# A transformer block with eight experts on one core: the experts' second product as three fp32r products in place of one fp32 product

## The chip, the cores and the metric

The kernel runs on one core of a Trainium2 chip. The time is that of one execution on the device, in microseconds (us). All times of instructions below come from one profiled execution.

## What is computed

The input is x, 4 batches of 1,024 rows of 128 numbers (4,096 tokens). After a layer norm with scale and shift, attention with 16 heads, a second layer norm and a router, every token goes to two of eight experts; each expert takes at most 1,280 rows. An expert is

```python
pre = jnp.einsum('ech,edh->ecd', expert_inputs, ff_pre_act_weight)
gate = jnp.einsum('ech,edh->ecd', expert_inputs, gate_weight)
expert_out = jnp.einsum('ecd,ehd->ech', pre * jax.nn.silu(gate), ff_post_act_weight)
```

with c = 1,280 rows, h = 128 and d = 512. The outputs are weighted, added up per token, multiplied by a gate and added to x. All of it is float32. The change concerns the last einsum alone, called the second product below; the first two are the gate product and the up product.

## The kernel before, in words

The program is written out by hand for each engine, and the engines meet at semaphores. Until 740 us it does the norms, the attention and the router; then come the eight experts, and after them a last stage that gathers the sums and writes the output. Only the expert stage is touched.

An expert e works on its rows in three parts n = 0, 1, 2 of 512, 512 and 256 rows (`CH`, line 36), and on its 512 hidden numbers in four pieces f of 128 (`FC`, line 35). Buffers alternate: q = e % 2 for weights and rows, f % 2 for the silu's result, and the two PSUM banks of the up and gate products.

TensorE (`expert`, line 1075) does, for each expert: `up(e, q, 0)`, `up(e, q, 1)`, `down` of part 0, `up(e, q, 2)`, the transposes of the next expert's rows for its parts 0 and 1 (`turn_rows`, line 1041), `down` of part 1, the transposes for part 2, `down` of part 2. It does not stop between two experts: `up(e + 1)` stands right behind.

- `up` (line 1050) makes, for each f, the gate product and then the up product. So an f is six fp32r matmuls (line 1047) with the weights as the stationary operand, 128 columns wide, and 512 or 256 rows moving. The gate product of f waits for the silu of f - 2, the up product of f for the hidden product of f - 2, since two PSUM banks of each are there.
- `down` (line 1064) is the second product: for each tile of 128 rows, four fp32 matmuls (line 1071) over f add up in PSUM. The hidden numbers of the tile are the stationary operand (128 columns), the 128 columns of w2 move. It waits for `hid_ready`, the hidden product of the part's last f, and for `y_ready`, that the PSUM bank was read. The trace shows each of these fp32 matmuls as two instructions, each with a weight load of its own (320 in the program, 640 in the trace).

ScalarE (`expert`, line 1255): for each f a silu of the gate product (line 1244, PSUM to `sg`, called hT in the trace); after a second product `results_out` (line 1251) weights its tiles into `yo`; it makes the high parts of the next expert's rows (line 1234) and, at the very end of expert e, of the first weights of expert e + 2 (`high_weights`, line 1223, 1,024 columns).

VectorE (`expert`, line 1749): for each f the hidden product hid = up x silu (line 1747, one operand in PSUM, one in SBUF), then the low parts of the next expert's rows (line 1729).

GpSimd (line 730): per expert ten indirect DMAs (line 725) that add a tile of 128 result rows each into the sums in DRAM, then `low_weights` (line 688), the low part of the first weights of expert e + 2, an SBUF subtraction of 1,024 columns. Ahead of the last stage it waits for nothing else; the last stage starts when the last of these DMAs has landed (line 451).

SyncE (line 438) loads the weights and rows of expert e + 2. The second weights w2 go to columns 1,024 to 1,535 of `w_raw` (called early in the trace), once the last second product of expert e has read them (line 448).

## Time and profile before

| | |
|---|---|
| median of three runs | 979.72 us |
| the three runs | 968.63, 979.72, 982.14 us |
| profiled execution | 973.02 us |
| its span, first to last instruction | 971.3 us |
| TensorE busy | 729.5 us (75%) |
| VectorE busy | 567.2 us (58%) |
| ScalarE busy | 460.5 us (47%) |
| GpSimd busy | 394.0 us (41%) |
| mean granted TensorE clock | 0.84 of full speed |
| first gate product of expert 0 | starts at 740.3 us |
| last second product of expert 7 | ends at about 937.5 us |

The span is read from the first instruction's start to the last one's end. PE is TensorE's matmuls and PEld its weight loads, DVE is VectorE, ACT ScalarE, POOL GpSimd, SP and SPq SyncE and its DMA queue. The duration of a matmul runs from its issue to the end of its results, so the durations of neighbours overlap; what one costs in a stream is the distance from its start to the start of the next.

### The profile page before, as it was taken

What the parts mean: (1) busy time and instruction counts of PE and PEld (TensorE: products, weight loads), DVE (VectorE), ACT (ScalarE), POOL (GpSimd) and SP (SyncE); (2) the same over time, 40 slices, a digit from 0 to 9 for tenths busy, and PEclk for the clock granted to TensorE, in tenths of its full rate; (3) what the DMA queues carried; (4) which work ended last, traced back from release to release, by engine and by line L of the source; (5) the groups of instructions that cost most, each with busy time, mean ns of one, the idle gap of its engine ahead of it and who ended that gap; (6) DMA issues with size and microseconds to landing.
All of it is one profiled execution on the core that took longest, in us unless ns stands there. A gap on an engine that the chain in (4) does not pass through costs nothing.

```text
span 971.3 us, 17136 instructions
## 1 busy us (share of the span) xinstructions
PE 729.5 (75%) x5876; PEld 395.5 (41%) x5876; DVE 567.2 (58%) x1066; ACT 460.5 (47%) x903; POOL 394.0 (41%) x432
## 2 busy tenths in 40 slices
PE   4654888888978747879876897975306999999960
PEld 2331233333423212334321342321304889889850
DVE  6859578888878925787763787720512333333314
ACT  2440467767756515756533765563103444444420
POOL 5550121113432341253151343255460677777762
PEclk9875599999979757998865998795656999999985
DMA  4255633451100111001010100000014454443326
GB/s 119 78 170 166 120 72 70 89 104 35 35 16 21 46 33 37 19 17 35 28 38 15 33 3 2 1 21 26 0 39 110 85 89 87 86 86 38 28 28 178
DMA packets 68177, 55.97 MB, mean 58 GB/s; under 512 B 7040, under 2 KB 58752, under 8 KB 68096
## 3 DMA queue, kind: packets, MB, share of 16 engines
q1 hardware_dynamic: 54528, 45.40, 17.9%
q0 software_dynamic: 13568, 9.51, 7.0%
q8 instruction: 48, 0.79, 0.3%
q14 instruction: 33, 0.27, 0.1%
HBM read 29.19 MB, written 25.31 MB: 56 GB/s over the span
## 4 chain that ended last, share of the span: by engine, by line
PE 58%; DVE 12%; ACT 9%; issue 7%; DMA 5%; another core or an unknown queue 4%; POOL 3%; SPq 2%; DVEq 0%; ACTq 0%; POOLq 0%
PE psum L847 15%; PE psum L832 13%; PE psum L1047 11%; PE psum L1071 7%; ACT prob_all L1189 7%; PE psum L807 5%; DVE mx L1381 2%; DMA k_parts<-prob_all 2%; PE psum L856 2%; DVE xn L1322 1%; PE psum L815 1%; SPq L365 1%; POOL slot_rows L622 1%; PE psum L885 1%
## 5 line engine op out<-in xcount | busy, mean ns | idle before, releaser
L1189 ACT ACTIVATE prob_all<-psum 128x512 f32<-128x512 f32 x576 | 318.0, 598 | 247.0 <-PE psum L832 205.7
L1381 DVE TENSOR_REDUCE mx<-psum 128x2 f32<-128x1024 f32 (+3 forms) x384 | 347.3, 953 | 141.4 <-PE psum L815 58.4
L832 PE MATMUL psum<-stack 51*128 51x512 bf16 (+3 forms) x768 | 199.9, 362 | 83.9 <-ACT prob_all L1189 64.0
L637 POOL TENSOR_SCALAR_AFFINE_SELECT prob_all<-prob_all 128x512 f32<-128x512 f32 x128 | 79.0, 635 | 395.5 <-ACT prob_all L1189 395.5
L807 PE MATMUL psum<-stack 48*128 48x512 bf16 (+3 forms) x768 | 165.6, 370 | 20.5 <-DVE mx L1381 11.7
L847 PE MATMUL psum<-prob_all,vst 128*32 128x512 f32 (+3 forms) x1536 | 180.2, 570 | 0.3 <-POOL prob_all L637 0.2
L725 POOL DMA_INDIRECT sums<-ys,dest_of x80 | 124.0, 1550 | 80.9 <-ACT ys L1251 53.0
L832 PEld LDWEIGHTS psum<-stack 51*128 51x128 bf16 x768 | 49.3, 96 | 256.2 <-ACT prob_all L1189 189.6
L1747 DVE TENSOR_TENSOR hid<-psum,hT 128x512 f32<-128x512 f32 (+1 forms) x96 | 57.1, 602 | 93.5 <-ACT hT L1244 66.4
L815 PE MATMUL psum<-mask_k,mask_q 64*128 64x64 bf16 x1024 | 78.0, 202 | 7.2 <-issue 7.2
L1071 PE MATMUL psum<-early,hid 128*128 128x128 f32 x640 | 75.2, 275 | 0.0
L622 POOL DMA_INDIRECT slot_rows<-early,idxb x64 | 62.8, 981 | 29.4 <-issue 19.0
L1071 PEld LDWEIGHTS psum<-early,hid 128*128 128x128 f32 x640 | 73.9, 192 | 0.6
L1047 PE MATMUL psum<-x_h,w_h 128*128 128x512 f32 (+1 forms) x192 | 71.6, 373 | 2.3 <-DVE x_l L1729 1.0
L1244 ACT ACTIVATE hT<-psum 128x512 f32<-128x512 f32 (+1 forms) x96 | 49.8, 530 | 49.6 <-PE psum L1047 45.7
L815 PEld LDWEIGHTS psum<-mask_k,mask_q 64*128 64x128 bf16 x1024 | 59.1, 104 | 29.8 <-issue 15.8
L1047 PE MATMUL psum<-x_h,w_l 128*128 128x512 f32 (+1 forms) x192 | 68.4, 356 | 0.0
L1047 PE MATMUL psum<-x_l,w_h 128*128 128x512 f32 (+1 forms) x192 | 68.4, 356 | 0.0
L807 PEld LDWEIGHTS psum<-stack 48*128 48x128 bf16 x768 | 49.4, 98 | 42.1 <-DVE mx L1381 28.6
L847 PEld LDWEIGHTS psum<-prob_all,vst 128*32 128x32 f32 x1536 | 37.9, 117 | 56.9 <-issue 50.3
L1251 ACT ACTIVATE ys<-psum,weight_of 128x128 f32<-128x128 f32 x80 | 23.2, 367 | 58.3 <-PE psum L1071 58.3
L1729 DVE TENSOR_TENSOR x_l<-psum,x_h 128x512 fp32r<-128x512 f32 (+1 forms) x24 | 13.8, 599 | 58.1 <-ACT x_h L1234 58.1
(178 smaller groups left out, 684.9 us busy)
## 6 DMA issues: line engine op xcount, KB each, us to landing
slot_rows<-fill SPq DMA_DIRECT2D x4, 1300.0 KB, 11.2
vals<-slot_rows SPq DMA_DIRECT2D x8, 650.0 KB
stack<-q_parts SPq DMA_DIRECT2D x32, 96.0 KB
stack<-k_parts SPq DMA_DIRECT2D x32, 96.0 KB
xs<-x SPq DMA_DIRECT2D x4, 512.0 KB, 6.3
stack<-q_parts SPq DMA_DIRECT2D x32, 64.0 KB
stack<-k_parts SPq DMA_DIRECT2D x32, 64.0 KB
early<-w1T SPq DMA_DIRECT2D x8, 256.0 KB
```

Of the source, the lines that this page charges most:

```text
L622: nc.gpsimd.indirect_dma_start(slot_rows, bass.IndirectOffsetOnAxis(ap=idxb[:, k, t:t + 1], axis=0), rows[:, k, t, :], None, bounds_check= ...
L637: ins = nc.gpsimd.affine_select(out=v, in_=v, compare_op=ALU.is_ge, fill=0.0, base=0, pattern=[[0, GH], [1, P]], channel_multiplier=-1)
L725: nc.gpsimd.indirect_dma_start(sums, bass.IndirectOffsetOnAxis(ap=dest_of[q][:, st:st + 1], axis=0), yo[q][:, st, :], None, bounds_check=T ...
L807: mm = nc.tensor.matmul(o, qst[buf][r, hp, i * P:i * P + P], kst[buf][r, hp, k0:k0 + w], start=True, stop=not diag, skip_group_check=True)
L815: mm = nc.tensor.matmul(o, mask_q[r, e, j, :], mask_k[r, e, j, :], start=False, stop=j == 1, skip_group_check=True)
L832: mm = nc.tensor.matmul(psum[:, KB[s % 2], col:col + w], kst[buf][r, hp, kb * P:kb * P + P], qst[buf][r, hp, qc * 512 + q0:qc * 512 + q0 + ...
L847: mm = nc.tensor.matmul(psum[32 * h:32 * h + 32, PV, q0:q0 + w], vst[buf][:, kb, h, :], probs[k % NP][:, h, col:col + w], start=kind in (0 ...
L1047: mm = nc.tensor.matmul(out_ap, left[a], right[b], start=i == 0, stop=i == 2)
L1071: mm = nc.tensor.matmul(psum[:, 6 + par, i * P:i * P + P], hid[par][:, f, i * P:i * P + P], w_raw[q][:, c:c + D], start=f == 0, stop=f == ...
L1189: nc.scalar.activation(probs[kind % NP][:, h, :], psum[:, KB[s % 2], :], ACT.Exp, scale=SCALE).then_inc(exped, 1)
L1381: ins = nc.vector.tensor_reduce(mx[:, part, :, hp, i], psum[:, QB[u % 2]:QB[u % 2] + 2, col:col + w], AX.X, ALU.max)
L1747: nc.vector.tensor_tensor(hid[par][:, f, 0:ns * P], psum[:, 2 + 2 * (f % 2), 0:ns * P], sg[f % 2][:, 0:ns * P], ALU.mult).then_inc(hid_rea ...
```

## The change

The hidden numbers and w2 are split into high and low parts as the rows and the first weights are, and `down` makes three fp32r matmuls of 128 moving columns for each fp32 matmul, with the tiles, the order over f and the PSUM bank as they were:

```diff
-        hid = [sb(f"hid{i}", [P, FC, 512]) for i in range(2)]
+        hid = [sb(f"hid{i}", [P, 512]) for i in range(2)]
+        hid_h, hid_l = ([sb(f"hid_{n}{i}", [P, FC, 512], F32R) for i in range(2)] for n in "hl")
+        w2_h, w2_l = ([sb(f"w2_{n}{i}", [P, FC * D], F32R) for i in range(2)] for n in "hl")
...
-                    sp.wait_ge(down_mm, e * 3 + 3)
+                    sp.wait_ge(w2_low, e + 1)
                     load_second_weights(e + 2, q)
...
             def down(e, q, n, par):
                 s0, ns = CH[n]
-                pe.wait_ge(hid_ready, (e * 3 + n) * FC + FC)
+                pe.wait_ge(hid_low, (e * 3 + n) * FC + FC)
                 after(pe, y_ready, e * 3 + n - 1)
+                hids, w2s = (hid_h[par], hid_l[par]), (w2_h[q], w2_l[q])
                 for i in range(ns):
                     for f in range(FC):
-                        c = 2 * F + f * D
-                        mm = nc.tensor.matmul(psum[:, 6 + par, i * P:i * P + P], hid[par][:, f, i * P:i * P + P],
-                                              w_raw[q][:, c:c + D], start=f == 0, stop=f == FC - 1)
+                        for k, (a, c) in enumerate(((0, 0), (0, 1), (1, 0))):
+                            mm = nc.tensor.matmul(psum[:, 6 + par, i * P:i * P + P],
+                                                  hids[a][:, f, i * P:i * P + P], w2s[c][:, f * D:f * D + D],
+                                                  start=f == 0 and k == 0, stop=f == FC - 1 and k == 2)
                 mm.then_inc(down_mm, 1)
...
-                pe.wait_ge(w2_in[q], j * 16 + 16)
+                pe.wait_ge(w2_low, e + 1)
                 down(e, q, 0, q)
...
+            def high_second(e, q, k):
+                act.wait_ge(w2_in[q], k * 16 + 16)
+                act.sem_inc(act_waited, 1)
+                nc.scalar.activation(w2_h[q][:], w_raw[q][:, 2 * F:3 * F], ACT.Copy).then_inc(w2_high, 1)
...
+            def high_hidden(e, n, f, par):
+                ns = CH[n][1]
+                act.wait_ge(hid_ready, (e * 3 + n) * FC + f + 1)
+                if f == 0:
+                    after(act, down_mm, e * 3 + n - 1)
+                nc.scalar.activation(hid_h[par][:, f, 0:ns * P], hid[f % 2][:, 0:ns * P], ACT.Copy
+                                     ).then_inc(hid_high, 1)
...
                     nc.scalar.activation(sg[f % 2][:, 0:ns * P], psum[:, 3 + 2 * (f % 2), 0:ns * P], ACT.Silu
                                          ).then_inc(silu_ready, 1)
+                    if f:
+                        high_hidden(e, n, f - 1, par)
+                high_hidden(e, n, FC - 1, par)
...
+            def low_hidden(e, n, f, par):
+                ns = CH[n][1]
+                dve.wait_ge(hid_high, (e * 3 + n) * FC + f + 1)
+                nc.vector.tensor_tensor(hid_l[par][:, f, 0:ns * P], hid[f % 2][:, 0:ns * P],
+                                        hid_h[par][:, f, 0:ns * P].bitcast(F32), ALU.subtract).then_inc(hid_low, 1)
+            def low_second(e, q):
+                dve.wait_ge(w2_high, e + 1)
+                dve.sem_inc(dve_waited, 1)
+                nc.vector.tensor_tensor(w2_l[q][:], w_raw[q][:, 2 * F:3 * F], w2_h[q][:].bitcast(F32), ALU.subtract
+                                        ).then_inc(w2_low, 1)
...
+                    after(dve, hid_low, (e * 3 + n) * FC + f - 1)
...
+                if not (isinstance(j, int) and j == NE // 2 - 1):
+                    dve.wait_ge(down_mm, e * 3 + 3)
+                    low_second(e + 2, q)
```

`high_second` stands behind `high_weights` on ScalarE, for experts 0 and 1 ahead of the experts and for e + 2 at the end of expert e. `low_second` stands on VectorE ahead of expert 0 and at the end of each expert up to the sixth. `hid` is now one part of two alternating pieces.

TensorE, the start of `down` for part 0 of expert 0 (one row here is one fp32 matmul, `early` is w_raw with w2 in it). Before:

```order
L1071 MATMUL psum<-early,hid0 128x128 [waits hid_ready,w2_in0]
L1071 MATMUL psum<-early,hid0 128x128 x15
```

and after the change, the first six of its 48 rows:

```order
L1075 MATMUL psum<-w2_h0,hid_h0 128x128 [waits hid_low,w2_low]
L1075 MATMUL psum<-w2_l0,hid_h0 128x128
L1075 MATMUL psum<-w2_h0,hid_l0 128x128
L1075 MATMUL psum<-w2_h0,hid_h0 128x128
L1075 MATMUL psum<-w2_l0,hid_h0 128x128
L1075 MATMUL psum<-w2_h0,hid_l0 128x128
```

Sixteen fp32 matmuls have become 48 fp32r matmuls with 128 moving columns, and the wait is now for the low parts.

VectorE, part 0 of expert 0 (hT is the silu's result). Before:

```order
L1747 TENSOR_TENSOR hid0<-psum,hT0 128x512 [waits up_mm,silu_ready]
L1747 TENSOR_TENSOR hid0<-psum,hT1 128x512 [waits up_mm,silu_ready]
L1747 TENSOR_TENSOR hid0<-psum,hT0 128x512 [waits up_mm,silu_ready]
L1747 TENSOR_TENSOR hid0<-psum,hT1 128x512 [waits up_mm,silu_ready]
L1747 TENSOR_TENSOR hid1<-psum,hT0 128x512 [waits up_mm,silu_ready]
```

and after:

```order
L1776 TENSOR_TENSOR w2_l1<-early,w2_h1 128x512 [waits w2_high]
L1786 TENSOR_TENSOR hid0<-psum,hT0 128x512 [waits up_mm,silu_ready]
L1786 TENSOR_TENSOR hid1<-psum,hT1 128x512 [waits up_mm,silu_ready]
L1769 TENSOR_TENSOR hid_l0<-hid0,hid_h0 128x512 [waits hid_high]
L1786 TENSOR_TENSOR hid0<-psum,hT0 128x512 [waits hid_low,up_mm,silu_ready]
L1769 TENSOR_TENSOR hid_l0<-hid1,hid_h0 128x512 [waits hid_high]
L1786 TENSOR_TENSOR hid1<-psum,hT1 128x512 [waits hid_low,up_mm,silu_ready]
L1769 TENSOR_TENSOR hid_l0<-hid0,hid_h0 128x512 [waits hid_high]
L1769 TENSOR_TENSOR hid_l0<-hid1,hid_h0 128x512 [waits hid_high]
L1786 TENSOR_TENSOR hid0<-psum,hT0 128x512 [waits hid_low,up_mm,silu_ready]
```

Each hidden product has got a subtraction of two SBUF operands, one step behind it, and the last subtraction of a part stands ahead of the next part's first hidden product.

## Rows read from the trace of the kernel before

**Rows 1.** Busy time of each engine by stretch, in us, with the granted clock (PEclk).

```profile
core 0: us, PE busy (x) PEld busy (x) DVE busy (x) ACT busy (x) POOL busy (x), PEclk, DMA share, GB/s
...
820.00:840.00 20.00, 19.86 (x144) 18.39 (x142) 7.48 (x15) 7.94 (x20) 14.07 (x9) 1.00 0.38 57
```

**Rows 2.** Chain of work that ended last, through expert 4: start, us, what.

```profile
840.13 11.17 PE psum L1047 x48
851.30 3.58 PE psum L1071 x32
...
859.12 3.57 PE psum L1071 x32
...
862.91 1.79 PE psum L1071 x16
...
864.74 3.46 PE psum L1047 x14
```

**Rows 3.** Timeline of PE around a second product: start, us, engine, line, shapes.

```profile
776.85 0.39 PE L1047 MATMUL psum<-x_l,w_h 128*128 128x512 f32 x1
777.08 0.39 PE L1047 MATMUL psum<-x_h,w_l 128*128 128x512 f32 x1
777.30 3.73 PE L1071 MATMUL psum<-early,hid 128*128 128x128 f32 x32
...
780.99 0.28 PE L1047 MATMUL psum<-x_l,w_h 128*128 128x256 f32 x1
781.11 0.28 PE L1047 MATMUL psum<-x_h,w_l 128*128 128x256 f32 x1
```

**Rows 4.** Timeline, and busy time with granted clock, of the router's 8-column products.

```profile
298.71 1.95 PE L885 MATMUL psum<-rT_s,xn 128*128 128x8 f32 x16
...
695.01 3.58 PE L885 MATMUL psum<-rT_s,xn 128*128 128x8 f32 x16 [0.69 <-ACT xn L1171]
...
298.60:301.00 2.40, 2.40 (x23) 2.04 (x25) 1.51 (x2) 0.60 (x2) 2.34 (x5) 1.00 0.00 0
...
694.90:698.70 3.80, 3.58 (x16) 3.49 (x16) 0.07 (x1) 0.06 (x1) 3.80 (x2) 0.50 0.00 0
```

**Rows 5.** Weight loads of lines 1047 and 1071: duration in ns, min/median/max.

```profile
L1047 PEld LDWEIGHTS psum<-x_l,w_h x192: 187/188/333, 740.5 to 931.6; 128*128 128x128 f32 x192
...
L1071 PEld LDWEIGHTS psum<-early,hid x640: 187/192/192, 752.5 to 937.1; 128*128 128x128 f32 x160
```

**Rows 6.** Timeline of ACT and DVE where expert 2 begins.

```profile
790.94 0.63 ACT L1251 ACTIVATE ys<-psum,weight_of 128x128 f32<-128x128 f32 x2 [0.59 <-PE psum L1071]
791.46 1.06 ACT L1223 ACTIVATE w_h<-early 128x1024 fp32r<-128x1024 f32 x1
792.41 0.60 ACT L1244 ACTIVATE hT<-psum 128x512 f32<-128x512 f32 x1
...
793.06 0.69 DVE L1747 TENSOR_TENSOR hid<-psum,hT 128x512 f32<-128x512 f32 x1 [2.09 <-ACT hT L1244]
```

**Rows 7.** Groups of instructions: a VectorE operation with two SBUF operands of 512 columns.

```profile
L1608 DVE TENSOR_TENSOR early<-early,modrow 128x512 f32<-128x512 f32 x2 | 1.4, 694 | 0.1
```

**Rows 8.** Timeline of DVE and POOL at 273 us, and DVE's line 1399 over the span.

```profile
273.45 1.13 DVE L1399 SCALAR_TENSOR_TENSOR mres<-mx,mparts 128x32 f32<-128x32 f32 x1
...
273.35 1.18 POOL L592 TENSOR_TENSOR early<-early,modrow 128x512 f32<-128x512 f32 x1 [0.18 <-POOL early L588]
...
L1399 DVE SCALAR_TENSOR_TENSOR mres<-mx,mparts x16: 191/192/1128, 89.7 to 627.0; 128x32 f32<-128x32 f32 x16
```

**Rows 9.** Timeline of POOL and ACT in expert 2 and the last expert.

```profile
801.21 2.92 POOL L688 TENSOR_TENSOR w_l<-early,w_h 128x1024 fp32r<-128x1024 f32 x1
...
930.75 1.55 POOL L725 DMA_INDIRECT sums<-ys,dest_of  x1 [5.74 <-ACT ys L1251]
...
947.44 1.55 POOL L725 DMA_INDIRECT sums<-ys,dest_of  x1 [0.30 <-issue]
...
935.72 1.14 ACT L1251 ACTIVATE ys<-psum,weight_of 128x128 f32<-128x128 f32 x4 [3.49 <-PE psum L1071]
```

More of the change, by code:

```diff
@@ L309, in build @@
             sem(n) for n in ("up_mm", "silu_ready", "hid_ready", "down_mm", "y_ready"))
+        hid_high, hid_low, w2_high, w2_low = (sem(n) for n in ("hid_high", "hid_low", "w2_high", "w2_low"))
         w2_in = [sem(f"w2_in{i}") for i in range(2)]
@@ L1223, in high_weights @@
                 nc.scalar.activation(w_h[q][:], w_raw[q][:, 0:2 * F], ACT.Copy).then_inc(w_high, 1)
+            def high_second(e, q, k):
+                act.wait_ge(w2_in[q], k * 16 + 16)
+                act.sem_inc(act_waited, 1)
+                nc.scalar.activation(w2_h[q][:], w_raw[q][:, 2 * F:3 * F], ACT.Copy).then_inc(w2_high, 1)
             for q in range(2):
                 high_weights(q, q, 0)
+                high_second(q, q, 0)
             for half in range(2):
@@ L1235, in high_rows, with silu @@
                                      ).then_inc(x_high, 1)
-            def silu(e, n):
+            def high_hidden(e, n, f, par):
[5 more added lines that the diff above has]
+                                     ).then_inc(hid_high, 1)
+            def silu(e, n, par):
                 ns = CH[n][1]
@@ L1256, in expert @@
                 e = j * 2 + q
-                silu(e, 0)
-                silu(e, 1)
+                silu(e, 0, q)
+                silu(e, 1, 1 - q)
                 after(act, sent[q], j * (16 * ST))
@@ L1262, in expert @@
                 results_out(e, q, 0, q)
-                silu(e, 2)
+                silu(e, 2, q)
                 if not last:
@@ L1272, in expert @@
                     high_weights(e + 2, q, j + 1)
+                    high_second(e + 2, q, j + 1)
             for n in range(3):
@@ L1738, in keep_dests @@
                                         spare[:].unsqueeze(2), ALU.min).then_inc(dest_kept, 1)
+            def low_hidden(e, n, f, par):
[8 more added lines that the diff above has]
+                                        ).then_inc(w2_low, 1)
             def hidden(e, n, par):
                 ns = CH[n][1]
-                after(dve, down_mm, e * 3 + n - 1)
                 for f in range(FC):
@@ L1746, in hidden @@
                     dve.wait_ge(up_mm, (e * 3 + n) * FC + f + 1)
-                    nc.vector.tensor_tensor(hid[par][:, f, 0:ns * P], psum[:, 2 + 2 * (f % 2), 0:ns * P],
+                    after(dve, hid_low, (e * 3 + n) * FC + f - 1)
+                    nc.vector.tensor_tensor(hid[f % 2][:, 0:ns * P], psum[:, 2 + 2 * (f % 2), 0:ns * P],
                                             sg[f % 2][:, 0:ns * P], ALU.mult).then_inc(hid_ready, 1)
+                    if f:
+                        low_hidden(e, n, f - 1, par)
+                low_hidden(e, n, FC - 1, par)
             def expert(j, q, last):
@@ L1763, in _ @@
             keep_dests(0, 0, 0)
+            for q in range(2):
+                low_second(q, q)
             for q in range(2):
```

## The prediction

> **What bounds the kernel now.** I read the busy time by stretch first. In the expert stage TensorE is busy 19.86 of 20 us at the full clock (granted 1.00, which is 2.4 GHz), while VectorE has 7.48, ScalarE 7.94 and GpSimd 14.07 of 20 us [rows 1]. Then the chain that ended last: from one expert's first gate product (840.13) to the next one's (864.74) it is 24.61 us, nearly all on TensorE: 11.17 us for the 48 matmuls of two parts, second products of 3.58, 3.57 and 1.79 us [rows 2]. So what the change adds to TensorE's stream is added to the time, and what it adds to the other engines costs only where TensorE comes to wait for them. Behind the last expert it is GpSimd's DMAs, the last issued at 947.44, that set when the final stage may begin [rows 9].
>
> **The cost of one matmul.** The three second products of an expert hold 40 fp32 matmuls, 80 instructions, in 3.58 + 3.57 + 1.79 = 8.94 us, or 0.112 us each [rows 2]. After the change they are 120 instructions, each loading 128 columns of weights and moving 128 columns. The trace has no fp32r matmul of 128 moving columns, so I bound its pitch (start to start).
>
> With 512 moving columns fp32r starts every 0.227 us (776.85 to 777.08 to 777.30, half of 0.45), with 256 every 0.12 us [rows 3]. Going by that alone the pitch falls by 0.107 for 256 columns fewer, and at 128 it would be 0.12 - 0.054 = 0.066 us. That is the lower end.
>
> But there is a row in which hardly anything moves: the router's product loads 128 columns of fp32 weights and moves 8. Its 16 instructions take 1.95 us with the tail of the last one (256 ns is the duration of one), so (1.95 - 0.256) / 15 = 0.113 us apart at clock 1.00, the pace of the second product, which moves 128. At clock 0.50 (1.2 GHz) they are (3.58 - 0.38) / 15 = 0.213 us apart [rows 4]. The pace there doubles with the clock period and does not hang on what moves: it is the weight load that sets it. Line 1047's fp32r loads last as long as line 1071's fp32 loads, 188 and 192 ns [rows 5], so I take it that an fp32r load holds the array as long. Then a matmul of 128 columns goes at the pace of its load, at least 0.112 us. The 256-column fp32r pitch, 0.12, is the upper end of this reading (a shorter product should not take longer). I take 0.116, the middle of these near rows: 120 x 0.116 = 13.92 us in place of 8.94, +4.98 us for an expert. With 0.112 it is +4.5, with 0.12 +5.46.
>
> **The work on the other engines.** ScalarE gets twelve copies for each expert (eight of 512, four of 256 columns) and one of w2 of 512. A 512-column ScalarE operation is 0.60 us, and 1,024 columns from SBUF are 1.06 [rows 6]; I take 0.60 and 0.4, 7 us for an expert. VectorE gets as many subtractions. The nearest row, 512 columns with two SBUF operands, is 0.69 us [rows 7], 0.42 for half of it, 7.9 us for an expert. Both fit beside some 29.7 us of TensorE (VectorE 7.48 x 24.6/20 = 9.2 + 7.9, ScalarE 9.8 + 7). What counts is the pace inside `up`: for each f TensorE takes 6 x 0.227 = 1.36 us, ScalarE 1.2, VectorE 0.69 + 0.69 = 1.38, less some 0.1 where the second starts before the first has ended, plus a few hundredths where it waits for itself. So VectorE just keeps up. The two PSUM banks leave room: the hidden product ends 0.84 us behind its up product and is needed 2.04 us behind it (three products of 0.68), 1.2 us of slack for falling behind. In part 2 (256 columns, 0.71 us per f on TensorE) VectorE and ScalarE are slower than TensorE, but the first two f need no wait, and TensorE has the transposes and `down` of part 1 behind them. I cost it at 0.1 us.
>
> At an expert's beginning ScalarE is late already: results, then `high_weights`, then the first silu at 792.41, and VectorE's first hidden product ends at 793.75 [rows 6]. TensorE began at 790.94 and wants that result for the third up product at 790.94 + 5 x 0.68 = 794.3: 0.6 us to spare. The w2 copy puts 0.5 us in front of the silu, and `low_second`, which waits for that copy, another 0.2 in front of the hidden product. The margin is used up: I cost it at 0.2 us, 0.3 for an expert with the above.
>
> The w2 loads of SyncE come earlier than before, since they wait for the split of the old w2 and no longer for the last `down`; they have a whole expert's time to land, and cost nothing. If they were late, ScalarE would stand at the end of an expert, which TensorE would feel after 0.6 us. The first two splits lie in the idle time ahead of expert 0.
>
> **The lock between VectorE and GpSimd.** At 273.45 a VectorE operation on SBUF operands that otherwise takes 192 ns took 1.13 us, and ended with the GpSimd operation that had started 0.1 us ahead of it [rows 8]. By the Trainium skill, "SBUF — State Buffer", in the section on the two sides of SBUF, a VectorE operation with two SBUF inputs and a GpSimd operation that reads SBUF exclude each other for the whole instruction; the trace agrees with it at that row. The hidden products had one operand in PSUM; the new subtractions are such operations, and GpSimd's `low_weights` takes 2.92 us once an expert [rows 9]. It started 10.3 us behind the expert's first product at 790.94 and will start at about 7 us, since the ten DMAs ahead of it keep their pace while the expert gets longer: in the middle of part 1. One subtraction is held up for 1.5 to 2.9 us there, of which 1.2 is slack. I count nothing for the short case, and up to 1.7 us x 6 = 10 us in the range.
>
> **The sum.** Seven experts at 4.98 + 0.3 give 37.0. In the last expert only the first second product counts in full (16/40 of 4.98 = 2.0): behind it GpSimd sends ten tiles without a pause from 930.75 to 947.44 + 1.55, (947.44 - 930.75) / 9 = 1.855 us apart [rows 9]. The results of part 1 were ready at 935.72 + 1.14 = 936.86 and GpSimd came to them at 938.17; the later second product moves them by 2.0 us, 0.7 past that point. Total 37.0 + 2.0 + 0.7 = 39.7; I say 39. Against the profiled execution: 973.0 + 39 = 1012. It lies 6.7 us below the median of the runs (979.7), and between their lowest and highest, so I put the forecast halfway, at 1015. With pitches of 0.112 and 0.12 the addition is 35 and 43; with the lock in full 53. On runs from 968.6 to 982.1 that is 1002 to 1034 for this case.
>
> **Rivals.**
>
> 1. *The load hides behind the product, not slower.* Place: the 120 instructions of `down`. If a fp32r load takes half the time of an fp32 one in the array, the pitch follows the moving columns down to 0.066 us: 120 x 0.066 = 7.9 us, 1.0 less than now; eight experts give -8, the stalls of 0.3 us give back 2, 973 - 6 = 967 us, no change. It decides once the pitch is below 0.094, where less than 20 us (2%) are added: 2.6 us for an expert, 0.3 of it stalls. For it: fp32r halves its pitch from 512 to 256 columns [rows 3]. Against it: the equal durations of the loads and the 8-column rows [rows 4, 5]. The Trainium skill, "TensorE: Matmul & The Clock Gate", section on the back-to-back issue gap, gives about 81 ns for a load and a product of 128 columns in a stream; by it the sum would be 120 x 0.081 = 9.7 us, +0.8 for an expert, 979 us. The page does not say of which type; no row here has it for 4-byte operands.
> 2. *Short fp32r products are slow.* Nothing shows fp32r below 256 columns. If the pitch at 128 were that of 512, 0.227, an expert would take 27.2 - 8.9 = 18.3 us more: seven times that, 7.3 and 6 in the last expert, 2 of stalls, +143: 1116 us. For it speaks only that no row excludes it; the fall from 512 to 256 speaks against it.
> 3. *The subtractions wait for the indirect DMAs too.* GpSimd spends 1.55 of every 1.855 us on them, ten for an expert [rows 9]. If they held the same lock, VectorE would get one subtraction in for each: an f would take 1.86 in place of 1.36 us, 8 x 0.5 = 4 us for an expert and 1 more in part 2, 6.5 times over +32: 973 + 39 + 32 = 1044 us. Against: they read a column of indices, not the data; no row has a VectorE operation on SBUF operands beside one of line 725.
>
> **How the numbers follow.** The forecast has 0.75, rival 1 0.08, rival 2 0.07, rival 3 0.10. About 2% is what a measurement of this kernel can tell from no change. Rival 1 is split 0.02 faster and 0.06 same; 0.01 of the forecast, should pitch and stalls both come out below the bounds, is same too; the rest is slower, 0.91. The range takes the forecast's own (1002 to 1034) and goes up to 1048 to hold rival 3; rivals 1 and 2 stay out.
>
> **What would show it.** Right: line 1075's matmuls 0.112 to 0.12 us apart, 13.4 to 14.4 us of them in an expert; experts 29 to 30.5 us apart; hardly any idle time of TensorE in `up`; one subtraction of 2 us or more in each expert, beside line 688 of before. Wrong: a pitch near 0.07 or 0.23 (rivals 1, 2); subtractions with a median far over 0.69 us and TensorE waiting for VectorE in `up` (rival 3); a change ahead of 740 us or after the last DMA, where nothing was touched.

## The result, and the profile after

The changed kernel takes 1018.15 us (median of four runs, 1015.84 to 1020.24), the kernel before 979.3 (968.63 to 982.14, four runs). The ratio is 1.0408 [1.0361, 1.0454]: slower, 3 us from the forecast of 1015. Here and below the ratio and its 95% interval are worked out from the single executions, those that ran slow as a whole left out, and the ratio is not quite the quotient of two medians. The profiled execution took 1020.24 us with a span of 1018.5; before it was 973.02.

The 47.2 us between the two profiled executions have two parts. The first gate product of expert 0 starts at 749.7 in place of 740.3 us. These 9.4 us lie where nothing was changed: the last softmax is already 9.3 us later. In the other profiles of this study, whose edits touch the expert stage alone, the experts begin at 704 to 710 us on one chip, 733 to 746 on a second and 745 to 754 on a third. From there to the end the stage takes 268.8 in place of 231.0 us, +37.8. That is the part that the change made, and ratios below are taken against the kernel before on the same chip, whose median was 943.6, 974.6 and 978.7 us on these three.

Busy time of each engine by stretch, which answers to [rows 1]:

```profile
core 0: us, PE busy (x) PEld busy (x) DVE busy (x) ACT busy (x) POOL busy (x), PEclk, DMA share, GB/s
820.00:840.00 20.00, 19.93 (x165) 19.09 (x163) 12.09 (x21) 9.79 (x25) 10.15 (x7) 1.00 0.29 45
```

TensorE is as full as before (19.86) and at the same clock, so the longer expert is work on TensorE, not waiting. VectorE's busy time went up from 7.48 to 12.09. The chain that ended last, through expert 3 to the start of expert 4, shows which work (start, us, what):

```profile
840.26 11.68 PE psum L1050 x48
851.95 5.32 PE psum L1075 x48
...
861.57 5.31 PE psum L1075 x48
...
867.13 2.63 PE psum L1075 x24
869.76 2.80 PE psum L1050 x12
...
872.74 0.70 DVE hid L1786
...
873.49 8.06 PE psum L1050 x33
```

Where [rows 2] had second products of 3.58, 3.57 and 1.79 us, there are now 5.32, 5.31 and 2.63: 13.26 in place of 8.94, +4.32 for an expert. 13.26 us divided by 120 instructions are 0.1105 us; in the timeline of PE they start 0.11 us apart (the views leave numbers out of the names, so w2_h stands there as w_h):

```profile
895.00 0.28 PE L1075 MATMUL psum<-w_h,hid_h 128*128 128x128 f32 x1
895.11 0.28 PE L1075 MATMUL psum<-w_l,hid_h 128*128 128x128 f32 x1
895.22 0.28 PE L1075 MATMUL psum<-w_h,hid_l 128*128 128x128 f32 x1
```

Over all of line 1075's instructions at the full clock the mean distance of two starts is 0.1116 us, the same as line 1071's before. The first products went from 11.17 to 11.68 us; that is where TensorE now waits a little. From the start of expert 1 to that of expert 7 the mean distance is 29.46 us, before 24.60: +4.86, of which 0.54 are not the second products.

The groups of instructions on the other engines (busy us, mean ns of one | idle just before):

```profile
L1769 DVE TENSOR_TENSOR hid_l<-hid,hid_h 128x512 fp32r<-128x512 f32 (+1 forms) x96 | 72.3, 753 | 5.7 <-ACT hid_h L1255 2.4
...
L1255 ACT ACTIVATE hid_h<-hid 128x512 fp32r<-128x512 f32 (+1 forms) x96 | 53.5, 558 | 37.6 <-DVE hid L1786 37.3
```

That is 9.0 us of subtractions and 6.7 of copies for an expert. All of line 1769 by duration (min/median/max in ns):

```profile
L1769 DVE TENSOR_TENSOR hid_l<-hid,hid_h x96: 415/681/3186, 755.9 to 979.4; 128x512 fp32r<-128x512 f32 x64, 128x256 fp32r<-128x256 f32 x32
```

And the timeline of VectorE and GpSimd in expert 3:

```profile
850.24 3.19 DVE L1769 TENSOR_TENSOR hid_l<-hid,hid_h 128x512 fp32r<-128x512 f32 x1
853.56 0.69 DVE L1786 TENSOR_TENSOR hid<-psum,hT 128x512 f32<-128x512 f32 x1
...
849.91 2.96 POOL L691 TENSOR_TENSOR w_l<-early,w_h 128x1024 fp32r<-128x1024 f32 x1
```

A subtraction that takes 0.68 us otherwise took 3.19 and ended 0.56 us behind GpSimd's: it had waited for it. There is one such in each of six experts, 3.16 to 3.19 us long, and none besides. It is what [rows 8] showed on a smaller scale (1.13 in place of 0.19 us). TensorE doesn't stop there: the chain is on it from 840.26 to 857.27. GpSimd's instruction starts 9.8 us behind the expert's first product (849.91 - 840.1); the prediction had said 7.

### The profile page after: what moved, and what is told of

Read it like the earlier page. It is cut to its first block, busy times and chain, and to the rows that moved or that the text cites. A ratio compares the mean times of both kernels' runs of the same rounds, so it can differ in the third digit from the quotient of the medians.

```text
span 1018.5 us, 18038 instructions
## 1 busy us (share of the span) xinstructions
PE 777.7 (76%) x6196; PEld 432.0 (42%) x6196; DVE 636.6 (62%) x1170; ACT 509.5 (50%) x1007; POOL 395.5 (39%) x432
## 4 chain that ended last, share of the span: by engine, by line
PE 61%; DVE 10%; ACT 8%; issue 6%; DMA 5%; another core or an unknown queue 4%; SPq 3%; POOL 2%; DVEq 0%; ACTq 0%; POOLq 0%
PE psum L850 15%; PE psum L835 13%; PE psum L1050 11%; PE psum L1075 10%; ACT prob_all L1194 6%; PE psum L810 4%; DVE mx L1406 2%; DMA k_parts<-prob_all 2%; PE psum L859 2%; SPq L368 2%; PE psum L818 1%; POOL slot_rows L625 1%; PE psum L1044 1%; PE psum L888 1%
## 5 line engine op out<-in xcount | busy, mean ns | idle before, releaser
L835 PE MATMUL psum<-stack 51*128 51x512 bf16 (+3 forms) x768 | 202.0, 368 | 87.4 <-ACT prob_all L1194 68.1
L850 PE MATMUL psum<-prob_all,vst 128*32 128x512 f32 (+3 forms) x1536 | 184.5, 582 | 0.2 <-POOL prob_all L640 0.2
L1075 PE MATMUL psum<-w_h,hid_l 128*128 128x128 f32 x320 | 88.0, 275 | 0.0
L1075 PE MATMUL psum<-w_l,hid_h 128*128 128x128 f32 x320 | 88.0, 275 | 0.0
L1075 PE MATMUL psum<-w_h,hid_h 128*128 128x128 f32 x320 | 87.9, 275 | 0.0
L1769 DVE TENSOR_TENSOR hid_l<-hid,hid_h 128x512 fp32r<-128x512 f32 (+1 forms) x96 | 72.3, 753 | 5.7 <-ACT hid_h L1255 2.4
L1050 PE MATMUL psum<-x_h,w_h 128*128 128x512 f32 (+1 forms) x192 | 74.3, 387 | 1.8 <-DVE x_l L1754 1.0
L1255 ACT ACTIVATE hid_h<-hid 128x512 fp32r<-128x512 f32 (+1 forms) x96 | 53.5, 558 | 37.6 <-DVE hid L1786 37.3
L810 PEld LDWEIGHTS psum<-stack 48*128 48x128 bf16 x768 | 49.4, 98 | 44.5 <-DVE mx L1406 28.4
```

The costliest lines, as they stand in the source:

```text
L810: mm = nc.tensor.matmul(o, qst[buf][r, hp, i * P:i * P + P], kst[buf][r, hp, k0:k0 + w], start=True, stop=not diag, skip_group_check=True)
L835: mm = nc.tensor.matmul(psum[:, KB[s % 2], col:col + w], kst[buf][r, hp, kb * P:kb * P + P], qst[buf][r, hp, qc * 512 + q0:qc * 512 + q0 + ...
L850: mm = nc.tensor.matmul(psum[32 * h:32 * h + 32, PV, q0:q0 + w], vst[buf][:, kb, h, :], probs[k % NP][:, h, col:col + w], start=kind in (0 ...
L1050: mm = nc.tensor.matmul(out_ap, left[a], right[b], start=i == 0, stop=i == 2)
L1075: mm = nc.tensor.matmul(psum[:, 6 + par, i * P:i * P + P], hids[a][:, f, i * P:i * P + P], w2s[c][:, f * D:f * D + D], start=f == 0 and k ...
L1769: nc.vector.tensor_tensor(hid_l[par][:, f, 0:ns * P], hid[f % 2][:, 0:ns * P], hid_h[par][:, f, 0:ns * P].bitcast(F32), ALU.subtract).then ...
```

## The experiments

All of them keep the stages outside the experts as they are. The measure for the mechanism is the mean distance of two experts' starts, over experts 1 to 6 (24.60 us before, 29.46 after).

**One part alone: the splits without the third products.**

```diff
-                        for k, (a, c) in enumerate(((0, 0), (0, 1), (1, 0))):
-                            mm = nc.tensor.matmul(psum[:, 6 + par, i * P:i * P + P],
-                                                  hids[a][:, f, i * P:i * P + P], w2s[c][:, f * D:f * D + D],
-                                                  start=f == 0 and k == 0, stop=f == FC - 1 and k == 2)
+                        mm = nc.tensor.matmul(psum[:, 6 + par, i * P:i * P + P],
+                                              hids[0][:, f, i * P:i * P + P].bitcast(F32),
+                                              w2s[0][:, f * D:f * D + D].bitcast(F32),
+                                              start=f == 0, stop=f == FC - 1)
```

> The changed kernel with all its splits, waits and copies, but the second product is one fp32 product of the high parts alone (the low parts of the hidden numbers and of w2 are made and waited for, and left out of the product). Theory (TensorE's stream pays for the 120 loads): the second products fall back to 80 instructions at 0.112 us, 8.9 us for an expert, and only the stalls stay: experts about 25.2 us apart against 24.6 before and 29.55 in the changed kernel, time some 4 to 6 us over the kernel before (ratio near 1.005). Rival (the copies and subtractions on ScalarE and VectorE are what costs): stays near 1018, ratio 1.04.

It took 958.38 us, ratio 1.0171 [1.0110, 1.0232], with 27.44 us from expert to expert. That is 2.84 more than before although TensorE's instructions are the old ones, far more than a few tenths. The timeline of DVE and POOL shows the held subtraction:

```profile
826.05 4.13 DVE L1769 TENSOR_TENSOR hid_l<-hid,hid_h 128x512 fp32r<-128x512 f32 x1
...
826.70 2.92 POOL L691 TENSOR_TENSOR w_l<-early,w_h 128x1024 fp32r<-128x1024 f32 x1
```

and busy time by stretch what follows from it (columns as above):

```profile
833.00:835.00 2.00, 0.65 (x4) 0.42 (x3) 1.20 (x4) 1.69 (x8) 0.02 (x1) 1.00 0.00 0
835.00:838.00 3.00, 3.00 (x15) 3.00 (x15) 2.08 (x6) 1.82 (x6) 2.70 (x2) 0.50 0.26 22
```

The chain that ended last shows the way from one to the other:

```profile
826.05 4.14 DVE hid_l L1769
...
832.47 0.04 ACT hid_h L1255
...
833.25 0.88 ACT ys L1275 x3
834.13 0.28 ACT hT L1265
...
834.45 2.84 PE psum L1050 x12
```

VectorE's hidden products come late behind the held subtraction, ScalarE's copy of the last one with them, and behind that copy stand, in ScalarE's order, the results of part 0 and the silu that TensorE waits for. So in part 2 no matmul starts for 1.63 us (the usual distance there is 0.12; the end of the one before still counts as busy), in each of the six experts, and behind three of these stops the granted clock is half for 3.4 us (here 835.0 to 838.4). The experts with a stop alone are 26.7 us apart, those with the lower clock too 28.0 to 28.4. The lock costs nothing in the changed kernel and over 2 us an expert here, with the same GpSimd instruction at nearly the same distance from the expert's start (9.8 and 10.6 us). Two things differ: the cover, since the second product of part 0, which lies between part 1 and part 2, is 5.3 us long there and 3.6 here, and the held subtraction, 3.19 there and 4.13 here. No run has one without the other.

**The lock taken away, with and without the third products.** GpSimd's subtraction for experts 2 to 7 is cut to 8 columns, so the low part of their first weights is left out; in one kernel on the changed kernel, in the other on the one above.

```diff
-                nc.gpsimd.tensor_tensor(w_l[q][:], w_raw[q][:, 0:2 * F], w_h[q][:].bitcast(F32), ALU.subtract).then_inc(w_low, 1)
+                w = 2 * F if isinstance(e, int) and e < 2 else 8
+                nc.gpsimd.tensor_tensor(w_l[q][:, 0:w], w_raw[q][:, 0:w], w_h[q][:, 0:w].bitcast(F32), ALU.subtract).then_inc(w_low, 1)
```

> The changed kernel, but GpSimd's subtraction low_weights does 8 of its 1,024 columns for experts 2 to 7 (the rest of these low weights is left out), so that it holds no lock worth speaking of. Theory (in the changed kernel it blocks one hidden subtraction for 3.2 us, nearly all of it hidden by the two PSUM banks and by the second product of part 0): no subtraction over 1 us in the experts, experts 29.2 to 29.5 us apart in place of 29.5; time as the changed kernel's or up to 2 us less. Rival (the lock is a large part of the 39 us): over 6 us less.

> The kernel of e1_fp32_high (second product as one fp32 product of the high parts) with the same cut of GpSimd's subtraction to 8 columns (left out: the low parts in the second product, and the low weights from expert 2 on). In e1 each of six experts had TensorE standing for 1.63 us while a subtraction on VectorE took 4.13 us, and the granted clock fell to half three times behind it. Theory (lock): both go, experts 24.8 to 25.2 us apart, some 10 to 13 us less than e1, ratio to before 1.003 to 1.007. Rival (the stalls are VectorE's and ScalarE's pace): experts stay at 26.7 and more.

The first took 1013.15 us, ratio 1.0425 [1.0342, 1.0509], 29.46 us from expert to expert, exactly as with the lock. All its subtractions by duration:

```profile
L1770 DVE TENSOR_TENSOR hid_l<-hid,hid_h x96: 414/681/694, 744.8 to 967.9; 128x512 fp32r<-128x512 f32 x64, 128x256 fp32r<-128x256 f32 x32
```

The maximum fell from 3,186 to 694 ns and nothing got faster: in the changed kernel the lock is there and hidden. The second took 979.96 us, ratio 1.0043 [0.9999, 1.0087], 25.12 us. So the splits alone cost 0.52 us an expert, and the account closes: 24.60 + 0.52 + 4.32 for the second products is 29.44, against 29.46 measured.

**The lock in four pieces.** The kernel with one fp32 product of the high parts, and GpSimd's subtraction as four instructions of 256 columns, nothing left out of it.

```diff
-                nc.gpsimd.tensor_tensor(w_l[q][:], w_raw[q][:, 0:2 * F], w_h[q][:].bitcast(F32), ALU.subtract).then_inc(w_low, 1)
+                n = 2 * F // 4
+                for c in range(0, 2 * F, n):
+                    ins = nc.gpsimd.tensor_tensor(w_l[q][:, c:c + n], w_raw[q][:, c:c + n],
+                                                  w_h[q][:, c:c + n].bitcast(F32), ALU.subtract)
+                ins.then_inc(w_low, 1)
```

> The kernel of e1_fp32_high with GpSimd's subtraction whole, but issued as four instructions of 256 columns in place of one of 1,024 (only the low parts in the second product are left out). Theory (the lock is held for one instruction at a time): a blocked subtraction on VectorE takes at most about 0.7 us longer, which the two PSUM banks hide; experts 24.8 to 25.3 us apart, like e6. Rival (GpSimd goes from one instruction to the next without giving the lock away): 26.7 as in e1.

979.65 us, ratio 1.0062 [1.0019, 1.0106], 25.12 us: as without the lock. Timeline of DVE and POOL:

```profile
844.14 1.27 DVE L1773 TENSOR_TENSOR hid_l<-hid,hid_h 128x512 fp32r<-128x512 f32 x1
...
844.81 3.80 POOL L693 TENSOR_TENSOR w_l<-early,w_h 128x256 fp32r<-128x256 f32 x4
```

VectorE gets in between the pieces: two or three subtractions of 1.1 to 1.9 us stand in place of one of 4.13, GpSimd needs 3.80 in place of 2.92 us, and TensorE has no stop over 0.5 us.

**Fewer moving columns.** What sets the pace of the second product, the load or what moves? The two correction products get 64 of the 128 columns; the others are left out of the correction.

```diff
-                        for k, (a, c) in enumerate(((0, 0), (0, 1), (1, 0))):
-                            mm = nc.tensor.matmul(psum[:, 6 + par, i * P:i * P + P],
-                                                  hids[a][:, f, i * P:i * P + P], w2s[c][:, f * D:f * D + D],
+                        wide, narrow = (0, 0, D), ((0, 1, D // 2), (1, 0, D // 2))
+                        each = (wide, *narrow) if f < FC - 1 else (*narrow, wide)
+                        for k, (a, c, w) in enumerate(each):
+                            mm = nc.tensor.matmul(psum[:, 6 + par, i * P:i * P + w],
+                                                  hids[a][:, f, i * P:i * P + P], w2s[c][:, f * D:f * D + w],
```

> The changed kernel, but in the high x low and low x high products only 64 of the 128 columns of w2 move (the other half of these two products is left out); number and size of the weight loads are as they were. Theory (each instruction costs its load, 0.111 us): nothing moves, pitch 0.111, experts 29.5 us apart, ratio 1.04. Rival (cost goes with the moving columns, at 2.4 columns a ns): 80 of 120 instructions save 0.027 us, 2.1 us for an expert, 27.4 apart, some 16 us less, ratio 1.025.

Timeline of PE at the full clock:

```profile
849.90 0.30 PE L1077 MATMUL psum<-w_h,hid_h 128*128 128x128 f32 x1
850.04 0.24 PE L1077 MATMUL psum<-w_l,hid_h 128*128 128x64 f32 x1
850.12 0.28 PE L1077 MATMUL psum<-w_h,hid_l 128*128 128x64 f32 x1
850.23 0.31 PE L1077 MATMUL psum<-w_h,hid_h 128*128 128x128 f32 x1
```

Within a group of three the distances differ (0.14, 0.08 and 0.11 us), but a group takes 0.335 us (the median), 3 x 0.1117, as expected. But the kernel took 1034.95 us, ratio 1.0971 [1.0915, 1.1027], with 37.47 us an expert, which nobody had expected. Part of it is the lock again (2.25 us and more without a new matmul), most the clock: busy time by stretch has

```profile
800.00:820.00 20.00, 20.00 (x134) 20.00 (x133) 5.89 (x15) 6.57 (x20) 7.42 (x5) 0.73 0.16 14
```

TensorE never idle in these 20 us, and granted 0.73 on average. Whether the lock's stop brings the clock down, or the columns do, two more kernels tell apart, with one execution each: the lock is taken away as above, and 64 and 96 columns move. The second's edit is the same with `96` for `D // 2`.

> The kernel of e2_narrow (64 of 128 columns in the high x low and low x high products) with GpSimd's subtraction cut to 8 columns for experts 2 to 7. In e2 the granted clock fell to half during second products and experts were 37 us apart, with a stall of 2.3 us in each from the lock. Theory (the clock falls because TensorE moves fewer columns in the second product, with no idle time in it): it still falls there, experts 33 us apart or more. Rival (the stalls by the lock pulled the clock down): the clock stays at 1.00, experts 29.3 to 29.6 apart, since each instruction still costs its load.

> As e11, but 96 of the 128 columns move in the high x low and low x high products (a quarter of these two products is left out). Theory (each instruction costs its load): pitch 0.111 us at the full clock and experts 29.4 us apart if the clock holds. Rival (columns): 80 x 0.0133 = 1.07 us less for an expert, 28.4. Whether the clock holds is open; if it falls, the pitch at clock 1.00 is what is read.

With 64 columns it took 1061.74 us (before 978.7), 35.01 us an expert. Busy time by stretch, ahead of the fall and in it:

```profile
825.00:837.00 12.00, 12.00 (x71) 10.53 (x70) 9.73 (x15) 8.22 (x15) 3.33 (x3) 1.00 0.34 61
838.00:844.00 6.00, 6.00 (x30) 6.00 (x30) 1.32 (x4) 2.79 (x9) 1.78 (x2) 0.50 0.00 0
```

In the 12 us ahead of it TensorE wasn't idle, nor in it, and the clock fell to 1.2 GHz inside the second product all the same. With 96 columns it took 1023.57 us, the clock stayed at 1.00 from 758.0 us to 990.1 and the chain reads as in the changed kernel:

```profile
855.21 5.32 PE psum L1078 x48
...
864.86 5.31 PE psum L1078 x48
...
870.41 2.63 PE psum L1078 x24
```

A quarter of the columns of two products in three taken away changes no number of 5.32, 5.31 and 2.63. So the moving columns don't set the pace. What stays the same in all these runs is the load of 128 columns of weights; no run loads fewer with as few moving, so that it is the load, and not another floor under each instruction, is the simplest reading and not tested. With 64 columns the pace at the full clock is the same too, but the full clock isn't held.

**Another size: w2 stationary.** If an instruction with a load of 128 columns costs at least 0.11 us, 512 columns moving under one load should cost less for each column. Here w2 is loaded and up to 512 columns of the hidden numbers move; the result lies transposed in PSUM and is left so.

```diff
-                for i in range(ns):
-                    for f in range(FC):
-                        for k, (a, c) in enumerate(((0, 0), (0, 1), (1, 0))):
...
+                for f in range(FC):
+                    for k, (a, c) in enumerate(((0, 0), (0, 1), (1, 0))):
+                        mm = nc.tensor.matmul(psum[:, 6 + par, 0:ns * P], w2s[a][:, f * D:f * D + D],
+                                              hids[c][:, f, 0:ns * P],
...
```

> The changed kernel with the operands of the second product exchanged: w2 is the stationary one, the hidden numbers move, 512 or 256 rows at a time, so a part of 512 rows takes 12 instructions in place of 48 (the results stand transposed in PSUM and are sent so; turning them back is left out). Theory (loads): 12 x 0.227 x 2 + 12 x 0.12 = 6.9 us for an expert in place of 13.3, experts about 23.2 us apart, time about 970 (ratio 0.99), unless GpSimd's ten DMAs and its subtraction, some 21.5 us for an expert, come in the way. Rival (three passes are dearer than one fp32 product however they are laid out): stays above 1000.

947.31 us, ratio 1.0052 [1.0020, 1.0083], 26.11 us an expert. The second product itself came out as worked out: 12 instructions in 2.72 us, 0.227 each. The time did not (23.2 us an expert had been expected): with only 2.7 us between part 1 and part 2 no matmul starts for some 0.77 and then 1.63 us in each expert, and in four of the six experts the granted clock is half for 3.4 us behind it. The hidden product behind the held subtraction (3.66 us) begins right when that ends, and from there the chain goes over ScalarE's results and the silu as above; this kernel was not run without the lock.

**Another order: the split of w2 in the middle.** The 0.5 us at an expert's start should go if the copy and the subtraction of the next w2 stand behind part 1's silus and hidden products.

```diff
                 silu(e, 1, 1 - q)
+                if not last and not (isinstance(j, int) and j + q == 0):
+                    high_second(e + 1, 1 - q, j + q)
...
                     high_weights(e + 2, q, j + 1)
-                    high_second(e + 2, q, j + 1)
...
                 hidden(e, 1, 1 - q)
+                if not last and not (isinstance(j, int) and j + q == 0):
+                    dve.wait_ge(down_mm, e * 3)
+                    low_second(e + 1, 1 - q)
                 hidden(e, 2, q)
...
-                if not (isinstance(j, int) and j == NE // 2 - 1):
-                    dve.wait_ge(down_mm, e * 3 + 3)
-                    low_second(e + 2, q)
```

> The changed kernel, nothing left out, but the split of w2 for expert e + 2 stands in expert e + 1 behind its part 1 (ScalarE's copy behind the silus of part 1, VectorE's subtraction behind the hidden products of part 1, both while TensorE does the second product of part 0) in place of the end of expert e. Theory (the split of w2 delays the first silu and hidden product of an expert and costs TensorE some 0.4 us there): experts 29.1 to 29.2 us apart in place of 29.55, some 3 us less in all, within the noise of the time but seen in the trace. Rival (the stalls come from VectorE's pace within the parts): 29.55 stays.

975.06 us, ratio 1.0318 [1.0254, 1.0381], 29.01 us from expert to expert, 0.45 less than the changed kernel (29.1 to 29.2 had been expected). The intervals of the two ratios overlap, so the gain in time is not shown, only the shorter distance. With VectorE busier in the middle the lock is no longer wholly covered: in three of the experts TensorE has a stop of 0.6 to 1.0 us there.

**All the computation, w2 stationary, turned back.** The transposed result is copied to SBUF (`y_t`), turned back by ten TensorE transposes an expert, and then weighted; with the late split and GpSimd's four pieces.

```diff
+            def back(e, n, par):
+                pe.wait_ge(yt_ready, e * 3 + n + 1)
+                for i in range(CH[n][1]):
+                    mm = nc.tensor.transpose(psum[:, 6 + par, i * P:i * P + P], y_t[par][:, i * P:i * P + P], identf[:])
+                mm.then_inc(back_mm, 1)
...
+            def turned_out(e, n, par):
+                ns = CH[n][1]
+                act.wait_ge(down_mm, e * 3 + n + 1)
+                nc.scalar.activation(y_t[par][:, 0:ns * P], psum[:, 6 + par, 0:ns * P], ACT.Copy).then_inc(yt_ready, 1)
```

> All of the computation: the fp32r second product with w2 stationary and the hidden numbers moving (12 instructions for a part), its result copied to SBUF by ScalarE and turned back by ten TensorE transposes for an expert, the split of w2 later as in e4_late_split, GpSimd's subtraction in four pieces. TensorE for an expert: 15.7 (up) + 1.1 (next rows) - the 1.1 is in the 24.6 of before, so 24.6 - 8.94 + 6.9 + 1.1 = 23.7 us plus stalls. Theory (loads and lock explain all): experts 23.8 to 24.6 us apart, within 1% of the kernel before, 35 us and more under the changed kernel. Rival (ScalarE, now some 19 us for an expert and with a chain copy, transpose, copy, sets the pace): over 25.5 us, slower than before.

980.43 us, ratio 1.0066 [1.0032, 1.0101], 25.75 us an expert. The theory had 23.8 to 24.6 and missed; the rival, ScalarE's chain of copies, had over 25.5. Timeline of PE, DVE and POOL in expert 4:

```profile
872.32 0.44 PE L1050 MATMUL psum<-identf,vals 128*128 128x128 f32 x2 [1.79 <-DVE x_l L1784]
...
865.53 2.59 DVE L1799 TENSOR_TENSOR hid_l<-hid,hid_h 128x256 fp32r<-128x256 f32 x1
...
864.47 3.36 POOL L695 TENSOR_TENSOR w_l<-early,w_h 128x256 fp32r<-128x256 f32 x4
```

In five of the six experts TensorE stands some 2.2 us, since the next rows' low parts are late. By the chain that ended last they are late by both: a subtraction held for 2.59 us, over several of GpSimd's pieces, and then ScalarE's four results (1.13 us), which stand ahead of the next rows' high parts. Here VectorE didn't get in between them; what decides whether it does was not found out.

So the last version does away with the lock's partner instead: `low_weights` for experts 2 to 7 moves to VectorE, the transposes for part 2's rows go behind `down` of part 2, and ScalarE makes the high parts of the next rows ahead of the results of part 0 (VectorE's part of the split of w2 goes back to the end of an expert). Nothing is left out.

```diff
-                low_weights(q + 2, q)
...
+            def dve_low_weights(e, q):
+                dve.wait_ge(w_high, e + 1)
+                dve.sem_inc(dve_waited, 1)
+                nc.vector.tensor_tensor(w_l[q][:], w_raw[q][:, 0:2 * F], w_h[q][:].bitcast(F32), ALU.subtract
+                                        ).then_inc(w_low, 1)
...
                 down(e, q, 1, 1 - q)
+                down(e, q, 2, q)
                 if not last:
                     turn_rows(e + 1, 1 - q, 2)
-                down(e, q, 2, q)
+                back(e, 1, 1 - q)
```

> All of the computation, as e8_swapped_back, with three things moved: the low part of the next expert's first weights is made by VectorE behind its part 1 (GpSimd only sends, so nothing locks), the transposes of the next rows' part 2 stand behind the second product of part 2, and ScalarE makes the next rows' high parts ahead of the results of part 0. In e8 TensorE stood 2.2 us for each expert ahead of those transposes, waiting for x_l, and a subtraction was locked out for 2.6 us. Theory (lock and that wait are all that is left over TensorE's 23.7 us): experts 23.8 to 24.5 us apart, time 0 to 6 us under the kernel before (ratio 0.994 to 1.000). Rival (ScalarE and VectorE, at 19 and 20 us of work for an expert, set the pace by their order): over 24.8, ratio over 1.003.

972.66 us against 978.7 on the same chip, ratio 0.9944 [0.9903, 0.9985]: the only version below the kernel before, by half a per cent, and by the two ratios some four and a half under the changed kernel. Half a per cent is less than the 2% that were taken as no change, though the interval leaves 1 out; the trace agrees, with 225.4 us from the first gate product to the end where the kernel before has 231.0. Chain of waits through expert 4:

```profile
842.42 8.71 PE psum L1050 x36
851.12 2.72 PE psum L1083 x12
853.84 2.87 PE psum L1050 x24
...
858.02 4.19 PE psum L1083 x24
...
865.84 8.74 PE psum L1050 x36
```

An expert is 23.44 us, 1.16 less than before and a little under the 23.8 to 24.5 expected, with the same three products per fp32 product. Its second products take 2.72 + 4.19 = 6.91 us where the changed kernel has 13.26; the extra copies and transposes give part of that back. No stop of TensorE is over 0.5 us, and the clock is 1.00 from 747.6 to 935.3. Several things moved at once here, so what the lock and what the order gave is not told apart.

## Why the prediction was right

- **The pitch.** I said 0.116 us, the middle of 0.112 and 0.12; it is 0.1116 from start to start, so the lower of these ends holds, and of the others (0.066, 0.227) neither. The reading from [rows 4] was right: what 8 columns need under a load of 128, 128 columns need too, and the runs with 64 and 96 columns show the same 0.11. That it is the load itself stays a reading. The term was 4.98 us an expert and measured 4.32. 120 x (0.116 - 0.1116) = 0.53 of the miss of 0.66 is the pitch; the other 0.13 is that the chain's three stretches are a little shorter than their count times the pitch (5.32 against 48 x 0.1116 = 5.36). Rivals 1 and 2 are out by this number. The Trainium skill, "TensorE: Matmul & The Clock Gate", section on the back-to-back issue gap, gives about 81 ns for a load and a product of 128 columns; for the 4-byte operands of this kernel the trace has 112, and the measurement decides.
- **The stops.** I said 0.3 us an expert and it is 0.54: 0.52 by the run without third products. The place was right for most of it, the start of an expert. There the w2 copy and its subtraction stand ahead of the first hidden product, for which TensorE waits (timeline of ACT and DVE):

```profile
871.26 0.63 ACT L1234 ACTIVATE w_h<-early 128x512 fp32r<-128x512 f32 x1
...
872.04 0.69 DVE L1776 TENSOR_TENSOR w_l<-early,w_h 128x512 fp32r<-128x512 f32 x1 [3.09 <-ACT w_h L1234]
872.74 1.29 DVE L1786 TENSOR_TENSOR hid<-psum,hT 128x512 f32<-128x512 f32 x2
```

  The first hidden product began at 872.74, 3.1 us behind the expert's first product at 869.6; in [rows 6] it was 2.1 (793.06 - 790.94). I had taken the copy at 0.5 and the subtraction at 0.2 of delay, 0.7 in sum, and it is 1.0. The late split, which takes both away from there, won 0.45 us back (the first hidden product begins at 2.3 to 2.4 us there).
- **The lock.** It came in every expert for which GpSimd makes weights, the subtraction 3.2 us long in place of 0.68, so held up for 2.5 us, within the 1.5 to 2.9 that I had said, and cost nothing, as counted in the short case: the run without it is at the same 29.46. Two details of the step failed. It lies 9.8 us, not 7, behind the expert's start, since the DMAs ahead of it don't keep their pace: the fifth of each ten waits for part 1's results, which are later too, 2.3 to 2.45 us from expert 0 to 5 where it was 0.6 before:

```profile
839.42 1.55 POOL L728 DMA_INDIRECT sums<-ys,dest_of  x1 [2.44 <-ACT ys L1275]
```

  And the 1.2 us of slack I had reckoned with were not what hid it; the delay runs down during the 5.3 us of `down` for part 0, which the change itself had made longer. Where that is 3.6 or 2.7 us, a subtraction of 4.13 or 3.66 us stops TensorE.
- **The tail.** 2.7 us were predicted for the last expert and what follows it; 60.4 against 57.4 is +3.0. The last expert's DMAs run as the step says, GpSimd waiting once for part 1's results:

```profile
982.18 1.55 POOL L728 DMA_INDIRECT sums<-ys,dest_of  x1 [0.30 <-issue]
985.25 1.55 POOL L728 DMA_INDIRECT sums<-ys,dest_of  x1 [1.52 <-ACT ys L1275]
...
983.26 1.14 ACT L1275 ACTIVATE ys<-psum,weight_of 128x128 f32<-128x128 f32 x4 [3.94 <-PE psum L1075]
```

- **The sum.** 39.7 us were predicted for the stage, 37.8 measured: expert 0 +5.6 (4.3 of it its second products; for the rest, the full clock was granted only from 755.9 us, 6.2 us behind its first product, before 2.9), experts 1 to 6 +29.2 (31.7 by my terms), the last and the tail +3.0. The median rose by 38.9, which takes in what lies ahead of the experts. So the addition of 39 fits the medians better than it fits the stage, and that is in part luck: two misses of opposite sign, pitch and stops, and some 1 us that no term stood for. The 3 us by which the forecast is short are nearly all its base, 976 where the median is 979.3. Two sums were a little off: with a pitch of 0.112 the terms give 7 x 4.8 + 1.8 + 0.7 = 36.1 us, not 35, and with that the forecast's own range is 1004.7 to 1035.1, not 1002 to 1034; the result lies in either. Of the signs, the second products' 13.26 us by the chain lie just under the 13.4 to 14.4 named; the others came, the long subtraction in the six experts beside which GpSimd makes weights.
- **Rival 3** had the subtractions wait for GpSimd's DMAs. The maximum of 694 ns over 96 subtractions, 64 of which begin while one of the 80 DMA instructions runs, with only GpSimd's subtraction cut down, excludes it.

Open: what exactly starts the fall of the clock with 64 columns, whether the floor of 0.11 us is the load's, and why VectorE got in between GpSimd's pieces in one kernel and not in the other. The 9.4 us ahead of the experts were told apart from the change by their place alone.

## What to carry to other kernels

Before splitting an fp32 product into three of fp32r, look for a row in which hardly anything moves: its pitch was the floor under every instruction here. At 128 moving columns three cost 0.335 us where the fp32 product's two instructions cost 0.223; with 512 columns under each load three cost 0.68, or 0.17 for each 128, so load the operand that can serve many columns, and count the transposes and copies if the result comes out turned (here half a per cent was left).

A lock between two engines costs what the engine behind them can't cover, so the same GpSimd instruction cost nothing where TensorE's next work was 5.3 us long, and 2.3 us an expert (27.44 - 25.12, of it 1.6 the stop and the rest the lower clock behind it) where it was 3.6 us long and the subtraction was held longer: when such work is shortened, expect the hidden stall to come up.

## What the runs showed of the hardware that had not been expected

- fp32 and fp32r instructions that load 128 columns have the same mean pitch at 2.4 GHz: 0.1116 us with 128 moving columns of either, 0.113 with 8 (fp32), and 0.335 for three in which two move 64 or 96 (fp32r).
- The granted clock fell from 1.00 to 0.50 with TensorE busy 6.00 of 6.00 us and no idle time in the 12 us ahead, where two of three products moved 64 columns; with 96 it stayed at 1.00 from expert 1 to the last (one execution each). It cost 35.01 - 29.48 = 5.5 us an expert: the kernel with fewer columns is the slower one.
- A subtraction held by GpSimd ends 0.56 us behind GpSimd's instruction both times shown, also where the trace lets it start 0.65 us ahead of it (4.13 us). Cut in four, GpSimd's work let VectorE in (1.1 to 1.9 us each) in one kernel and held it for 2.59 us in another.
- The 1.55 us of an indirect DMA on GpSimd hold no such operation up: with the lock's partner cut down, 64 of the 96 subtractions begin beside one, and none took over 0.694 us.
